# A four-layer transformer kernel: the second layer in steps of two heads of both sequences, with output and down products turned around

## What is computed

```python
# x: (16, 256, 128); for each sequence
xn = layernorm(x)
q, k, v = split(xn @ w_qkv)                  # 16 heads of 64
att = softmax(q @ k.T + mask)                # causal, near or first 64
out = concat_heads(att @ v) @ w_out          # (1024 -> 128)
scores = sigmoid(xn @ gate_w.T)              # 8 experts
w = where(expert is in top 2 of scores, scores, 0)
moe = sum over e of square(relu((xn * w[e]) @ w_up[e].T)) @ w_down[e].T
x = x + out + moe
```

## Time and profile before

| what | value |
|---|---|
| time, three executions | 2084.85, 2078.9, 2081.28 us; median 2081.28 |
| the profiled execution | 2087.24 us, of it the span 2085.4 us |
| busy over the span | PE 1927.2 us (92%), DVE 1416.6 (68%), ACT 1175.8 (56%), POOL 884.5 (42%) |
| mean granted TensorE clock | 0.961 of full speed |
| second layer | 413.1 to 1172.4 us after the span's start |
| last layer | 1582.1 to 2083.0 us |
| square on GpSimd, 128x512 (L1606) | 1041 ns |
| weights of one unit on GpSimd (L1593) | 418 and 626 ns |

### The profile page before, as it was taken

The page is one execution under the profiler, slowest core; times in us unless marked ns, Lnnn a source line. Parts: engine busy times, 40 slices in busy tenths (PEclk is TensorE's granted clock), DMA queues, the critical chain, the costliest instruction groups (busy, mean ns, idle before and its releaser), DMA issues.

```text
span 2085.4 us, 45689 instructions
## 1 busy us (share of the span) xinstructions
PE 1927.2 (92%) x15332; PEld 1490.5 (71%) x15332; DVE 1416.6 (68%) x5247; ACT 1175.8 (56%) x3527; POOL 884.5 (42%) x1384
## 2 busy tenths in 40 slices
PE   5787887389999999999999999999998999999999
PEld 2565654268888888888888666666666777777777
DVE  6999963377767767776776666666663666666665
ACT  3444253155555655555565456555554777777776
POOL 3112365645555555555555411122113555555554
PEclk9889699689999999999999899999998999999999
DMA  6000015620000000000000000000000000000000
GB/s 191 25 2 1 2 33 121 159 92 2 2 2 2 2 1 2 2 2 2 2 1 2 1 1 1 1 1 1 1 1 1 2 7 7 7 7 6 7 5 9
DMA packets 40822, 37.08 MB, mean 18 GB/s; under 512 B 5904, under 2 KB 38800, under 8 KB 39696
## 3 DMA queue, kind: packets, MB, share of 16 engines
q1 hardware_dynamic: 34960, 29.82, 4.5%
q0 software_dynamic: 5632, 4.33, 1.5%
HBM read 23.53 MB, written 10.62 MB: 16 GB/s over the span
## 4 chain that ended last, share of the span: by engine, by line
PE 67%; DVE 9%; issue 3%; ACT 2%; POOL 1%; DMA 0%; POOLq 0%; DVEq 0%; ACTq 0%
PE bank L1357 5%; PE bank L1335 4%; PE bank L2214 4%; PE bank L1322 4%; PE bank L2201 3%; PE bank L1261 3%; PE bank L1308 3%; PE bank L2225 3%; PE bank L2189 3%; PE bank L1305 3%; PE bank L2186 2%; PE bank L1720 2%; PE bank L1246 2%; PE bank L1791 2%; PE bank L1248 2%
## 5 line engine op out<-in xcount | busy, mean ns | idle before, releaser
L1593 POOL TENSOR_TENSOR work<-work 128x128 f32<-128x128 f32 (+1 forms) x524 | 257.0, 522 | 357.1 <-DVE work L1521 357.1
L2398 POOL TENSOR_TENSOR work<-work 128x128 f32<-128x128 f32 (+1 forms) x512 | 243.7, 509 | 232.2 <-DVE work L2341 232.1
L1388 ACT ACTIVATE work<-work 128x128 f32<-128x128 f32 x262 | 103.3, 394 | 274.5 <-DVE work L1507 274.5
L2346 DVE COPY work<-bank 128x384 f32<-128x384 f32 x256 | 134.4, 547 | 34.3 <-PE bank L2214 33.6
L1516 DVE COPY work<-bank 128x384 f32<-128x384 f32 x260 | 140.2, 544 | 6.6 <-issue 0.4
L2336 DVE CUSTOM_DVE_ANT_0 work<-bank,mask 128x128 f32<-128x128 f32 x256 | 73.5, 287 | 90.7 <-PE bank L2189 90.6
L1357 PE MATMUL bank<-w_l,work 128*128 128x128 f32 x1024 | 134.9, 275 | 0.0
L2259 ACT ACTIVATE work<-work 128x128 f32<-128x128 f32 x256 | 100.7, 393 | 60.0 <-DVE work L2337 60.0
L1606 POOL TENSOR_TENSOR work<-work 128x512 f32<-128x512 f32 x129 | 134.3, 1041 | 0.0
L1389 ACT ACTIVATE work<-work 128x256 f32<-128x256 f32 x262 | 129.3, 494 | 0.0
L2260 ACT ACTIVATE work<-work 128x256 f32<-128x256 f32 x256 | 127.0, 496 | 0.0
(11 more groups left out here) (384 smaller groups left out, 5891.0 us busy)
## 6 DMA issues: line engine op xcount, KB each, us to landing
w_l<-in_l SPq DMA_DIRECT2D x1, 3210.5 KB, 13.0
w_l<-in_l SPq DMA_DIRECT2D x2, 1540.0 KB
w_f<-in_f SPq DMA_DIRECT2D x1, 3072.0 KB, 13.5
x_sb<-in_x SPq DMA_DIRECT2D x4, 512.0 KB, 7.0
normed_rows<-work SPq DMA_DIRECT2D x1, 2048.0 KB, 9.3
even_experts<-x_sb SPq DMA_DIRECT2D x8, 256.0 KB, 3.6
residual<-x_sb SPq DMA_DIRECT2D x1, 2048.0 KB, 8.6
qk<-in_qk SPq DMA_DIRECT2D x2, 1024.0 KB, 4.8
```

The costliest lines, as they stand in the source:

```text
L1593: ins = pool.tensor_tensor(w, w, spread(rc[:, g % 4, q:q + 1], w.shape[1]), ALU.mult)
L2346: dve.tensor_copy(pt[u], PS[u][:, 0:384]).then_inc(s_te.s, 1)
L2398: ins_ = pool.tensor_tensor(w, w, spread(rc[:, g % 2, u, q:q + 1], w.shape[1]), ALU.mult)
```

## The change

The second layer is written anew (`second_layer`) after the last layer's pattern: 8 passes of 8 steps, two heads of both sequences per step, four units, the ring of two banks, no step of a pass that doesn't exist.
- Output and down: the weights are stationary and 512 tokens stream; both are added up in bank 5, features by tokens, over a pass and all experts. One expert is worked per step for both sequences.
- So the gate must be applied by token before the down product: it is multiplied in together with the ReLU, by VectorE (`gated`, one operation on 128 x 512 out of PSUM), and GpSimd squares. ScalarE's ReLU and VectorE's two additions per step go.
- For that the gates must lie along the free dimension, the same on all partitions: TensorE turns them (32 rows of 128), ScalarE copies them out, SP writes them to DRAM, and eight loads per pass bring each expert's row back to all 128 partitions.
- At a pass's end ScalarE copies bank 5, TensorE turns it back in four transposes, and VectorE adds it to x.
- The ring's list now has queries, keys, two up projections and values in each step, and once per pass the turned x ("t"), logits ("g"), turned gates ("w") and the sum turned back ("b").
- The weights of the later layers are loaded behind the first pass's gates. The last layer changes only in how its semaphore counts are taken over.

```diff
@@ second layer: the old attention() goes, second_layer() comes
+            ITEMS = [("t", 0), ("g", 0), ("w", 0)]
+            for s in range(-1, N + 4):
+                if 0 <= s < N:
+                    ITEMS.append(("q", s))
+                if s >= 0 and (s + 1) % PAIRS == 0 and s + 1 < N:
+                    ITEMS.append(("g", (s + 1) // PAIRS))
+                if 0 <= s < N:
+                    ITEMS.append(("k", s))
+                if 0 <= s - 2 < N:
+                    ITEMS += [("u", 2 * (s - 2)), ("u", 2 * (s - 2) + 1)]
+                if s > 0 and s % PAIRS == 0 and s < N:
+                    ITEMS.append(("w", s // PAIRS))
+                if s >= 0 and (s + 2) % PAIRS == 0 and s + 2 < N:
+                    ITEMS.append(("t", (s + 2) // PAIRS))
+                if s >= 11 and (s - 11) % PAIRS == 0:
+                    ITEMS.append(("b", (s - 11) // PAIRS))
+                if s + 1 < N:
+                    ITEMS.append(("v", s + 1))
...
+            def pe_(pe):
+                def ring(kind, n):
+                    m = place[kind, n]
+                    if m >= 2:
+                        taken(pe, *ITEMS[m - 2])
+                    return bank_of(kind, n)
...
+                def output(g):
+                    i, j = divmod(g, PAIRS)
+                    if j == 0:
+                        past(pe, y_s, i)
+                    past(pe, s_ot, g + 1)
+                    pe.matmul(ACC[:, :], L["wout"][:, j * 128:(j + 1) * 128], ot[g % 2], start=(j == 0), stop=False,
+                              skip_group_check=True).then_inc(o_f.s, 1)
...
+                def down(g):
+                    e = g % PAIRS
+                    past(pe, f_q, 2 * g + 2)
+                    for c in range(2):
+                        mm = pe.matmul(ACC[:, :], L["down"][:, (2 * e + c) * D:(2 * e + c + 1) * D], h2[c], start=False, stop=(e == PAIRS - 1 and c == 1),
+                                       skip_group_check=True)
+                    mm.then_inc(f_d.s, 1)
...
+                for s in range(-1, N + 4):
+                    if 0 <= s - 1 < N:
+                        scores(s - 1)
+                    if 0 <= s - 3 < N:
+                        weighted(s - 3)
+                    if 0 <= s - 2 < N:
+                        turned(s - 2, 0)
+                        turned(s - 2, 1)
+                    if 0 <= s < N:
+                        project("q", s)
+                    if 0 <= s - 2 < N:
+                        turned(s - 2, 2)
+                        turned(s - 2, 3)
+                    if s >= 0 and (s + 1) % PAIRS == 0 and s + 1 < N:
+                        logits((s + 1) // PAIRS)
+                    if 0 <= s < N:
+                        project("k", s)
+                    if 0 <= s - 3 < N:
+                        output(s - 3)
+                    if 0 <= s - 2 < N:
+                        up(2 * (s - 2))
+                    if 0 <= s - 3 < N:
+                        down(s - 3)
+                    if 0 <= s - 2 < N:
+                        up(2 * (s - 2) + 1)
+                    if s > 0 and s % PAIRS == 0 and s < N:
+                        gates_turned(s // PAIRS)
+                    if s >= 0 and (s + 2) % PAIRS == 0 and s + 2 < N:
+                        turn((s + 2) // PAIRS)
+                    if s >= 11 and (s - 11) % PAIRS == 0:
+                        turned_back((s - 11) // PAIRS)
+                    if s + 1 < N:
+                        values(s + 1)
...
+                def gated(u):
...
+                    dve.wait_ge(g_in[e // 2], 32 * (i + 1))
+                    past(dve, f_q, u - 1)
+                    dve.scalar_tensor_tensor(hs[c], bank_of("u", u)[:, :], 0.0, gate[e].rearrange("p t k -> p (t k)"), ALU.max,
+                                             ALU.mult).then_inc(f_h.s, 1)
...
+                for s in range(-1, N + 4):
+                    i, at = divmod(s + 4, PAIRS)
...
+                    if s in (-1, 0):
+                        experts_added(dve, s + 2)
+                    if 0 <= s - 2 < N:
+                        gated(2 * (s - 2))
+                    if 0 < i < PASSES:
+                        if at == 0:
+                            if i == 1:
+                                dve.wait_ge(x_sum, len(ACC_TILES))
+                            moments(i)
+                        if at == 1:
+                            normed(i)
+                        if at == 2:
+                            rest(i)
+                        if at == 3:
+                            gates(i)
+                    if 0 <= s - 2 < N:
+                        gated(2 * (s - 2) + 1)
+                    if s >= 11 and (s - 11) % PAIRS == 0:
+                        added((s - 11) // PAIRS)
...
+            def sp_(sp):
+                sp.wait_ge(phase_end, 4)
+                sp.wait_ge(x_sum, len(ACC_TILES))
                 for i in range(PASSES):
...
+                    past(sp, r_act, act_rank[place["w", i]] + 1)
+                    sp.dma_start(gates_d[i % 2], wT[0:4 * E1]).then_inc(g_out, 16)
+                    sp.wait_ge(g_out, 16 * (i + 1))
+                    for e in range(E1):
+                        past(sp, f_h, 2 * (PAIRS * (i - 1) + e) + 2)
+                        sp.dma_start(gate[e], gates_d[i % 2].rearrange("(t e) k -> e t k", e=E1)[e].unsqueeze(0).to_broadcast([128, 4, 128])).then_inc(g_in[e // 2], 16)
```

More of the change, by code:

```diff
@@ L1136, in attention @@
             xn_at = top[0]
[L1137 to L1138 removed]
+            carve(4, 512)
+            x_hi, x_lo = ([rounded(f"l1_{part}_{p}", "work", xn_at + (2 * n + p) * 512, 512) for p in range(2)]
                           for n, part in enumerate(("xn_hi", "xn_lo")))
[L1142 to L1146 removed]
@@ L1198, in misc_at @@
-            def misc_at(i, kind, n, full, back=0):
-                f, e, place = shared[BANK[kind]]
-                N = len(place)
-                while (kind, n) not in place:
-                    n, back = (n + PER[kind], back - N) if n < min(m for k, m in place if k == kind) else (n - PER[kind], back + N)
-                sm_ = f if full else e
-                return sm_.s, sm_.at(i, place[kind, n] + back)
-            def made(i, kind, n):
-                return misc_at(i, kind, n, True)
@@ new lines, in second_layer, with bank_of, values_of @@
+            place = {what: n for n, what in enumerate(ITEMS)}
+            act_kinds = [kind not in "ub" for kind, _ in ITEMS]
+            act_rank = [sum(act_kinds[:n]) for n in range(len(ITEMS))]
+            def bank_of(kind, n):
+                return RING[place[kind, n] % 2]
+            def values_of(c):
+                i, c = divmod(c, PAIRS)
+                return i, c // 4, c % 4
+            r_full, r_act = Count(a_A, B, len(ITEMS)), Count(a_xse, B, sum(act_kinds))
+            s_f, s_mx, s_ex = Count(a_s, 2 * B, UNITS * N), Count(a_sub, 2 * B, UNITS * N), Count(a_exp, 2 * B, UNITS * N)
@@ L1641, in program @@
         pre_q = sem("pre_q")
-        attention("l1", 1, "qk1", mask1, "l1", 2, False)
+        second_layer()
         def layer2():
```

738 lines of the change are left out of this document (291 added, 447 removed).

## The result

The changed kernel takes 2068.81 us (median of six runs) against 2082.53 of the kernel before in six runs beside it: a ratio of 0.9942, 95% interval 0.9928 to 0.9956. By that ratio it is 12.1 us less (9 to 15); the two medians lie 13.7 apart. I had forecast no measurable change, 2082.6. The range (2066 to 2098) holds the result, but the kernel became faster by more than its interval, which I had not forecast. The profiled execution took 2069.05 us with a span of 2067.2.

What follows compares the result with a forecast made beforehand. TensorE was taken to bound the second layer: steps, extra work, waits, filling and draining summed to 754.7 us against 759.3 (-4.6); 5.9 for the clock made +1.3, so a median of 2082.6 us, range 2066 to 2098.

Steps and rivals of the forecast that it cites:

- The plain step: TensorE's work in one second-layer step without extra items, summed from trace pieces: 10.74 us, eight steps 85.9.
- the last rival: Output and down: 512-column FP32 products cost more than read, 19 us per 0.1 us on three products; no chance given.
- The clock: TensorE's granted clock may fall after the 2.8 us wait in seven passes: 0 to 11.9 us, half taken.
- I take half, 5.9: Time added to the second layer for TensorE clock falls, midway between 0 and 11.9 us.
- the rival on the slower side: TensorE's clock falls after the wait for x_lo in every pass: +7.3 us, 2088.6; chance 0.36.
- The waits: TensorE's values wait for the second gated copy in steps with extra items: 2.8, 0.9, 0.65, 0.5, together 4.85 us per pass.
- Making the gates: Nine VectorE operations between the gated copies in step s = 7: 3.1 to 5.2 us, taken as 4.2.
- my middle value: VectorE's time for making the gates, 4.2 us between 3.1 and 5.2, as only one GpSimd square falls there.
- Filling and draining: Second layer's start up to full steps 32.35 us, its end 22.35 us.
- +1.3: Forecast change of the second layer in us: -4.6 from the sum, with 5.9 for the clock.
- Faster because the waits are short: Rival: no fall of TensorE's clock and gates at 3.1 us, hidden: -8.1 us, 2073; chance 0.19.
- The order costs nothing: Rival: the subtraction and late gated copies on VectorE are covered, 34 us go: 2047; chance 0.07.

Runs made afterwards that it cites:

- split128: The changed kernel with each 512-column output and down product issued as four of 128 columns, weights still stationary; ratio to the kernel before 0.9980, plain step 10.59 us.
- output_first: The changed kernel with the output product issued ahead of the keys' projection on TensorE; ratio to the kernel before 0.9948, plain step 10.50 us.
- the two filled kernels: The changed kernel with 18 or 10 unread identity products ahead of the values in the step that turns x; ratios to the kernel before 0.9939 and 0.9903.

## Why the prediction was wrong

**The plain step failed**, the sum "1.51 + 1.45 + 0.63 + 0.78 + 1.36 + 0.86 + 1.56 + 1.72 + 0.87 = 10.74". Each piece was a true reading from start to start, but not the price of its group alone. A rounded group behind transposes holds 0.08 us of them, and their own row is as much too short (split128 and output_first). In the earlier trace rows queries, keys and values all stand behind transposes. I priced both up projections like the queries (0.78) and the values at 0.87; in the new step the up projections stand behind products of 512 columns and the values behind an up projection, and they come to 0.69 (1.55 - 0.86), 0.69 (2.41 - 1.72) and 0.79 (the last of the three values' products is 0.33 ahead of the scores, here as in the last layer, which makes the other 0.1). So 0.08 us of transposes that were already in the sum were counted three times more: 10.74 instead of 10.49, 0.25 per step, over 61 steps 15.2 us, over twice what can be measured. The 512-column form of the output and down products, whose price I had doubted in the last rival, was priced rightly (0.03 forecast for each, 0.10 for three measured).

**The clock** was half right. "I take half, 5.9": it fell in six of seven passes, 6 x 1.6 = 9.6, so 3.7 more. The trigger named, idle TensorE in that wait, is shown by the two filled kernels; that it lay at six of seven and not at half was not to be read from any row before. The Trainium skill, TensorE: Matmul & The Clock Gate, "HAM oscillation", has such a kernel pay the slow clock in every round; the rows of this case agree in 41 of 49 passes. I had that mechanism as the rival on the slower side; it came, and the cheaper step outweighed it.

**The waits** were right: 4.81 against 4.85 per pass, each at its place, released by VectorE's gated copy. One detail moved: the late gates cost nothing in their own step and 0.3 us in the next. **Making the gates** took 4.06 us up to the gated copy behind them (forecast 4.2). VectorE, then GpSimd in the pass shown:

```profile
584.41 0.42 DVE L1463 TENSOR_TENSOR w_l<-work 128x256 f32<-128x256 f32 x1
584.87 1.26 DVE L1464 TENSOR_TENSOR w_l<-w_l,w_const 128x256 f32<-128x256 f32 x1
586.17 0.43 DVE L1465 TENSOR_TENSOR w_l<-work 128x256 f32<-128x256 f32 x1
```
```profile
584.81 1.04 POOL L1556 TENSOR_TENSOR work<-work 128x512 f32<-128x512 f32 x1 [1.97 <-PE bank L1303]
```

The one operation that meets GpSimd's square takes 1.26 us and ends 0.28 behind it, its neighbours of the same size 0.42. The Trainium skill, SBUF — State Buffer, "Who interferes with whom", says that VectorE's operations with two SBUF inputs contend with GpSimd's that read SBUF, under an exclusive lock; the row agrees, and my middle value held because only one of the nine operations meets a square. At the layer's start, with no square beside them, the nine took 3.31 us from the first start to the last end, in the passes 4.14.

**Filling and draining** were right: 32.0 us against 32.35, 22.6 against 22.35.

The forecast by these steps: +1.3 - 15.2 + 3.7 - 0.1 = -10.3 us, which is the layer's change.

**The rivals.** "Faster because the waits are short" had the right sign by the wrong mechanism: no wait was short. "The order costs nothing", 2047, had about the right size for what the order costs, though not by its parts: it priced the waits alone at 34 us and no fall of the clock. Moving the items gives 0.9761, which is 2032.7 us with the kernel before at 2082.53; that is 49.8 us less than before and 36 less than the change.

## What to carry to other kernels

Price matmuls from start to start only as a whole stretch. A piece cut out of it can hold the end of the piece before (here 0.08 us behind transposes), and put together with other neighbours it counts that end again; a tenth of a microsecond per step of a loop decides the sign. Check by adding neighbours: here the sum over them stayed when the order changed. A wait of TensorE inside dense work costs itself and, mostly, a fall of the clock (here 2.5 + 1.6 us): it is the first thing to look for after such a change, by asking what stands between an engine's copy and the bank that it frees. An extra item in a ring of two banks makes the item two behind it wait for that one's reader, so it belongs where the reader is long done.

## What the runs showed that I had not expected

- The record of a rounded product starts about 0.03 us after the start of the FP32 instruction ahead of it, however long that one takes. So the same group of three reads 0.78 behind transposes or short FP32 products and 0.70 behind rounded ones, and nothing was gained or lost by the order.
- Which operand of FP32 products of 128 columns is stationary made no difference: 10.59 us per step with the weights kept, 10.60 with the tokens changing.
- About 2.2 us of useless products in each of seven waits took 9.9 us off the layer, as the clock did not fall.
- A broadcast of 256 KB from DRAM lands after 6.1 us, a 256 KB store from SBUF after 3.6.
- The first layer's end spread over 13 us (405 to 418) between executions, the second layer's length over 0.3.
